# Six early chunks of a head-attention kernel: summing two tiles' products on TensorE and multiplying a third on VectorE

## The reference, cut to what matters

```python
q = (Q @ Wq.T + bq).reshape(n, ql, 16, 8)          # Q = layernorm(x)
k = (K @ Wk.T + bk).reshape(n, ql, 16, 8)          # K = V = context
v = (V @ Wv.T + bv).reshape(n, ql, 16, 8)
attn = softmax(einsum('nlhd,nled->nlhe', q, k) / sqrt(8), axis=-1)
ctx = einsum('nlhe,nled->nlhd', attn, v).reshape(n, ql, 128)
x = x + tanh(g) * (ctx @ Wo.T + bo)
```

## Time and profile before

| | |
|---|---|
| median of 3 runs | 1273.81 us (1272.21 to 1274.23) |
| the profiled execution | 1265.46 us, of which the span of the instructions is 1263.7 us |
| busy over the span | TensorE 89%, VectorE 76%, GpSimd 55%, ScalarE 54% |
| attention of the first six chunks | from 14.5 us (first product) to 227.1 us (first product of the seventh chunk) |
| 118.4 to 152.9 us, one chunk of these | TensorE busy 33.32, VectorE 32.16, GpSimd 33.12, ScalarE 14.84 of 34.50 us |
| 600 to 1260 us | TensorE busy 635.3 of 660 us |

### The profile page before, as it was taken

How to read it: one execution, slowest core, us unless ns; L and a number is a source line. 1 busy time by engine, 2 the same in 40 slices (tenths; PEclk the granted TensorE clock), 3 DMA queues, 4 the chain that set the end, 5 groups by cost and what they waited for, 6 DMA issues and landing times.

```text
span 1263.7 us, 23900 instructions
## 1 busy us (share of the span) xinstructions
PE 1124.9 (89%) x7368; PEld 965.1 (76%) x7368; DVE 957.1 (76%) x2069; ACT 682.0 (54%) x1939; POOL 692.6 (55%) x424
## 2 busy tenths in 40 slices
PE   5579974799889998896999999999999999999998
PEld 2356552688779887785989999999788888888886
DVE  4999999899999999988546444445867777777765
ACT  4434442466566765553564555555455555555554
POOL 6889997989899998988331010101133333333311
PEclk9975555799999999898899999999999999999999
DMA  3733432888779886877675566561111111111100
GB/s 109 241 116 126 133 109 93 250 251 250 238 226 280 258 251 206 245 246 223 204 240 163 167 185 187 186 191 61 34 33 34 34 35 35 33 35 34 33 9 18
DMA packets 134840, 183.34 MB, mean 145 GB/s; under 512 B 11293, under 2 KB 69176, under 8 KB 134714
## 3 DMA queue, kind: packets, MB, share of 16 engines
q1 hardware_dynamic: 129594, 169.22, 43.3%
q0 software_dynamic: 5120, 12.59, 2.9%
HBM read 146.10 MB, written 35.66 MB: 144 GB/s over the span
## 4 chain that ended last, share of the span: by engine, by line
PE 54%; DVE 26%; POOL 8%; issue 7%; ACT 3%; DMA 0%; DVEq 0%; POOLq 0%; ACTq 0%
PE ZB L1437 7%; DVE q_sb L1044 6%; PE YB L1451 6%; PE YD L1492 5%; DVE s L1019 4%; PE ZD L1403 4%; PE ZD L1405 4%; PE ZD L1404 4%; PE YB L1492 3%; POOL prod L635 3%; POOL prod L647 3%; PE ZB L1403 2%; DVE own_prod L1008 2%; DVE own_prod L1000 2%; PE ZB L1405 2%
## 5 line engine op out<-in xcount | busy, mean ns | idle before, releaser
L772 ACT ACTIVATE hid<-ZB,w2b 128x128 f32<-128x128 f32 x768 | 217.0, 374 | 110.2 <-PE YB L1451 72.5
L635 POOL TENSOR_TENSOR prod<-q_sb,kv_sb 128x2048 f32<-128x2048 f32 x48 | 216.0, 4502 | 36.6 <-DVE q_sb L1044 27.3
L1437 PE MATMUL ZB<-bt,w1b 128*128 128x128 f32 x1536 | 213.9, 284 | 23.8 <-ACT hid L772 17.9
L647 POOL TENSOR_TENSOR prod<-s,kv_sb 128x2048 f32<-128x2048 f32 x48 | 215.2, 4504 | 9.8 <-DVE q_sb L1044 9.6
L1437 PEld LDWEIGHTS ZB<-bt,w1b 128*128 128x128 f32 x1536 | 196.0, 199 | 29.8 <-issue 28.9
L622 POOL TENSOR_TENSOR rstd<-ve,neghalf 128x4 f32<-128x4 f32 x64 | 66.4, 1037 | 266.2 <-DVE ve L962 264.9
L679 POOL TENSOR_TENSOR own_prod<-own_prod,prod 128x512 f32<-128x512 f32 x44 | 56.5, 1284 | 205.3 <-ACT prod L804 205.3
L1451 PE MATMUL YB<-w2b,hid 128*128 128x128 f32 x1024 | 142.3, 283 | 0.0
L1246 DVE TENSOR_TENSOR prod<-own_prod,ZD 128x512 f32<-128x512 f32 x102 | 70.0, 686 | 93.4 <-ACT own_prod L794 52.1
L1451 PEld LDWEIGHTS YB<-w2b,hid 128*128 128x128 f32 x1024 | 130.5, 196 | 7.3 <-ACT hid L772 0.2
L794 ACT ACTIVATE own_prod<-ZD 128x512 f32<-128x512 f32 x102 | 61.0, 598 | 97.9 <-PE ZD L1405 97.3
(11 more groups left out here) (274 smaller groups left out, 2436.7 us busy)
## 6 DMA issues: line engine op xcount, KB each, us to landing
w2b<-in_w SPq DMA_DIRECT2D x96, 516.0 KB
w1b<-in_w SPq DMA_DIRECT2D x96, 512.0 KB, 4.9
xb<-xs SPq DMA_DIRECT2D x96, 128.0 KB, 3.4
ctx_t<-in_ctx SPq DMA_DIRECT2D x24, 256.0 KB, 3.1
x2d<-x2s SPq DMA_DIRECT2D x48, 128.0 KB, 5.0
x<-in_x SPq DMA_DIRECT2D x16, 256.0 KB, 3.6
xs<-zrow SPq DMA_DIRECT2D x4, 1024.0 KB, 6.0
xrow<-in_x SPq DMA_DIRECT2D x16, 256.0 KB, 5.1
```

Of the source, the lines that this page charges most:

```text
L635: pool.tensor_tensor(out=prod[:, t % 2, :].rearrange("p (h e d) -> p h e d", h=HEADS, e=HEADS), in0=q.unsqueeze(2).broadcast_to([P, HEADS, ...
L647: pool.tensor_tensor(out=prod[:, (t + 1) % 2, :].rearrange("p (h d e) -> p h d e", h=HEADS, e=HEADS), in0=s0[:, t, :, :].unsqueeze(2).broa ...
L772: act.activation(hid[n % 2][:, j, k * RT:(k + 1) * RT], ZB[j // 2][:, at:at + RT], ACT.Relu, bias=w2b[t % 3][:, k, e, FJ * D + j:FJ * D + ...
L1437: last = pe.matmul(ZB[j // 2][:, at:at + RT], w1b[t % 2][:, k, e, j * P:(j + 1) * P], bt[t % 2][:, k * RT:(k + 1) * RT], start=True, stop= ...
```

## The change

In the first six chunks (`EARLY = 6`):

- TensorE sums the products of tiles 0 and 1. It multiplies the slices of `prod` by the identity and lets PSUM add them up: for the scores 8 calls per tile on 256 columns each, taken 8 elements apart (`sum_scores`, at k = 3 and 5), for the outputs 16 calls per tile on 128 columns each, taken 16 elements apart (`sum_outputs`, at k = 11 and 12). All are full fp32 matmuls, which the program issues as two instructions each. The sums stand in ZD0 and ZD1.
- VectorE no longer sums these four. It takes maxima, subtraction and scaling of tiles 0 and 1 from PSUM, and does the first pair's maxima at k = 7 instead of k = 5 (ScalarE's exponential moves from k = 6 to k = 7).
- VectorE makes tile 2's product with the values (`second_times_v`) instead of GpSimd, from a copy of these values in YB, in `own_prod`, sums it, and then uses `own_prod` for tile 3. It adds a copy of 128 x 128 at k = 15.
- GpSimd makes five products per chunk instead of six. The two buffers alternate over the whole row of products.
- The languages stand at (0, 2, 7, 9) instead of (0, 2, 9, 12), and with them their loads and stores on SyncE.

The diff, cut to its core:

```diff
-LANG_AT = [16 * (c // 4) + 31 + (0, 2, 9, 12)[c % 4] for c in range(NC)]
+LANG_AT = [16 * (c // 4) + 31 + (0, 2, 7, 9)[c % 4] for c in range(NC)]
...
+EARLY = 6
+def product_buffer(a, i):
+    return (5 * a + i) % 2 if a < EARLY else i % 2
...
             def times_k(a, t):
                 if t == 2:
                     emptied(pool, "kv1", a)
-                    pool.wait_ge(score0.sem, score0.at(a, 1))
+                    if a < EARLY:
+                        pool.wait_ge(pe_sk.sem, pe_sk.at(a, 1))
+                    else:
+                        pool.wait_ge(score0.sem, score0.at(a, 1))
+                elif has(a - 1) and a - 1 < EARLY:
+                    pool.wait_ge(pe_sv.sem, pe_sv.at(a - 1, 1 + t))
...
             def times_v(a, t):
                 pool.wait_ge(exp0.sem, exp0.at(a, 1 + t // 2))
-                if t < 2:
+                if a < EARLY and t == 0:
+                    pool.wait_ge(pe_sk.sem, pe_sk.at(a))
+                elif t < 2:
                     pool.wait_ge(score0.sem, score0.at(a, 2 + t))
...
-                if k in (8, 10, 12) and has(a):
+                if k in (8, 10, 12) and has(a) and (a >= EARLY or k < 12):
                     times_v(a, k // 2 - 4)
...
+            def second_times_v(a):
+                dve.wait_ge(exp0.sem, exp0.at(a, 2))
+                dve.wait_ge(score0.sem, score0.at(a))
+                v = values_two.rearrange("p (d e) -> p d e", e=HEADS)
+                dve.tensor_tensor(out=own_prod[:].rearrange("p (h d e) -> p h d e", h=HEADS, e=HEADS),
+                                  in0=s0[:, 2, :, :].unsqueeze(2).broadcast_to([P, HEADS, HD, HEADS]),
+                                  in1=v.unsqueeze(1).broadcast_to([P, HEADS, HD, HEADS]),
+                                  op=ALU.mult).then_inc(two_av.sem, 1)
...
+            def sum_scores(a, t):
+                pe.wait_ge(pool_qk.sem, pool_qk.at(a, t + 1))
+                if has(a - 1):
+                    pe.wait_ge(sub0.sem, sub0.at(a - 1, 2))
+                src = prod[:, product_buffer(a, t), :].rearrange("p (g d) -> p g d", d=HD)
+                n = HEADS * HEADS
+                for d in range(HD):
+                    last = pe.matmul(pe_scores[:, t * n:(t + 1) * n], ident[:], src[:, :, d], start=(d == 0), stop=(d == HD - 1))
+                last.then_inc(pe_sk.sem, 1)
+
+            def sum_outputs(a, t):
+                pe.wait_ge(pool_av.sem, pool_av.at(a, t + 1))
+                if has(a - 1):
+                    pe.wait_ge(o_ready.sem, o_ready.at(a - 1, 1))
+                src = prod[:, product_buffer(a, 3 + t), :].rearrange("p (g e) -> p g e", e=HEADS)
+                for e in range(HEADS):
+                    last = pe.matmul(pe_outputs[:, t * D:(t + 1) * D], ident[:], src[:, :, e], start=(e == 0), stop=(e == HEADS - 1))
+                last.then_inc(pe_sv.sem, 1)
...
+                s, k = a_part(half)
+                if k in (3, 5) and 0 <= s < EARLY:
+                    sum_scores(s, k // 2 - 1)
+                if k in (11, 12) and 0 <= s < EARLY:
+                    sum_outputs(s, k - 11)
                 if half in LANG:
                     languages(LANG[half])
```

More of the change, by code:

```diff
@@ L368, in build @@
         sum_bank = [YB, ZD[1]]
+        pe_scores, pe_outputs, values_two = ZD[0], ZD[1], YB[:, 0:D]
         def tiles(b):
@@ L829, in _ @@
                     normed(0, lambda j: xn0[:, j, :], lambda j: x0[:, j, :], p, (0, 1) if k == 5 else (2, 3))
-                if k == 6 and has(a):
+                if k == 6 and a >= EARLY and has(a):
                     exp_heads(a, 0)
@@ L833, in _ @@
                     keys_values(p, 1)
+                if k == 7 and 0 <= a < EARLY:
+                    exp_heads(a, 0)
                 if half == 14:
@@ L1033, in head_sum @@
                 dve.wait_ge(exp0.sem, exp0.at(a, pair + 1))
+                if pair == 0 and a < EARLY:
+                    dve.tensor_reduce(out=rec0, in_=s0[:, ts, :, :].rearrange("p t h e -> p (t h) e"), axis=X, op=ALU.add).then_inc(rec0_s.sem, 1)
+                    dve.wait_ge(rec0_s.sem, rec0_s.at(a, 1))
+                    dve.reciprocal(rec_early[:], rec0).then_inc(rec0_s.sem, 1)
+                    return
                 dve.tensor_reduce(out=sum0[:, ts, :], in_=s0[:, ts, :, :], axis=X, op=ALU.add).then_inc(rec0_s.sem, 1)
@@ L1038, in head_out @@
             def head_out(a, t):
-                if t < PT:
+                second = t == 2 and a < EARLY
+                if second:
+                    dve.wait_ge(two_av.sem, two_av.at(a))
+                elif t < PT:
                     dve.wait_ge(pool_av.sem, pool_av.at(a, t + 1))
@@ L1042, in head_out @@
                     dve.wait_ge(own_av.sem, own_av.at(a))
-                src = prod[:, (t + 1) % 2, :] if t < PT else own_prod[:]
+                src = prod[:, (t + 1) % 2, :] if t < PT and not second else own_prod[:]
                 dve.tensor_reduce(out=o_sb[a % 2][:, t, :], in_=src.rearrange("p (g e) -> p g e", e=HEADS),
-                                  axis=X, op=ALU.add).then_inc(av_sum.sem, 1)
+                                  axis=X, op=ALU.add).then_inc(av_sum.sem, 3 if a < EARLY and t == 2 else 1)
             def head_scale(a, pair):
                 ts = slice(2 * pair, 2 * pair + 2)
-                dve.wait_ge(av_sum.sem, av_sum.at(a, 2 * pair + 2))
                 dve.wait_ge(rec0_s.sem, rec0_s.at(a, 2 * pair + 2))
                 o = o_sb[a % 2][:, ts, :].rearrange("p t (h d) -> p (t h) d", h=HEADS)
-                dve.tensor_tensor(out=o, in0=o, in1=rec0.unsqueeze(2).broadcast_to([P, 2 * HEADS, HD]),
+                if pair == 0 and a < EARLY:
+                    dve.wait_ge(pe_sv.sem, pe_sv.at(a))
+                    src, rec = pe_outputs[:, 0:2 * D].rearrange("p (g d) -> p g d", d=HD), rec_early[:]
+                else:
+                    dve.wait_ge(av_sum.sem, av_sum.at(a, 2 * pair + 2))
+                    src, rec = o, rec0
+                dve.tensor_tensor(out=o, in0=src, in1=rec.unsqueeze(2).broadcast_to([P, 2 * HEADS, HD]),
                                   op=ALU.mult).then_inc(o_ready.sem, 1)
@@ L1283, in _ @@
                     later_consts()
-                if k == 0 and has(r):
+                if k == 0 and r >= EARLY and has(r):
                     head_out(r, 2)
@@ L1292, in _ @@
                         variances_of_rows(p)
-                if k == 3 and has(a):
+                if k == 3 and a >= EARLY and has(a):
                     head_scores(a, 0)
-                if k == 4 and has(a):
+                if k == 4 and a >= EARLY and has(a):
                     head_scores(a, 1)
-                if k == 5 and has(a):
+                if k == 5 and a >= EARLY and has(a):
                     head_max(a, 0)
@@ L1302, in _ @@
                     norm_stats(1, lambda j: row[:, j, 0:D], r)
+                if k == 7 and 0 <= a < EARLY:
+                    head_max(a, 0)
                 if k == 7 and has(a):
@@ L1311, in _ @@
                     head_sum(a, 0)
-                if k == 11 and has(a):
+                if k == 11 and a >= EARLY and has(a):
                     head_out(a, 0)
@@ L1315, in _ @@
                     pick_group(r)
-                if k == 13 and has(a):
+                if k == 13 and a >= EARLY and has(a):
                     head_out(a, 1)
+                if k == 13 and 0 <= a < EARLY:
+                    second_times_v(a)
+                if k == 14 and 0 <= a < EARLY:
+                    head_out(a, 2)
                 if k == 14 and has(a):
```

35 lines of the change are left out of this document (26 added, 9 removed).

## The result

The changed kernel takes **1341.83 us** (median of 4 runs, 1339.86 to 1347.51) against 1273.01 us of the kernel before (4 runs, 1271.57 to 1274.23): ratio 1.0548, 95% interval 1.0513 to 1.0583. It is 69 us slower. The forecast was 1281 us; rival C, at 1342 us, is what came. The profiled execution took 1342.77 us, with a span of 1341.0.

What follows compares the result with a forecast made beforehand. GpSimd was taken to set the pace, 34.5 us per chunk. Start +1.3, two middle intervals +3.2 and the table interval +2.5 made +7 us, so the median 1273.8 became 1281 us; range 1258 to 1345.

Steps and rivals of the forecast that it cites:

- rival C: TensorE's sums read spaced columns at half speed at the high clock, 7.1 to 7.8 us each: +68, 1342 us; chance 0.14.
- case A: Main case: the forecast's sum of terms over the six chunks, +0 to +20 us, with borrowed sum prices; chance 0.57.
- The price of the sums: On TensorE at clock 1.00: 3.9 us per sum of scores, 3.6 per sum of outputs, 15 us per chunk.
- the ring: GpSimd and TensorE waiting on each other round a chunk: 19.8 + 16.3 = 36.1 us where it was 34.5, +1.6.
- The clock: TensorE's granted clock was taken as high (1.00) from the first chunk on, where it had been 0.50.
- D: Rival: TensorE's clock stays at 0.50, 61.7 us of work per chunk: +127, 1401 us; chance 0.09.
- K2: GpSimd's third key product, which may start only after TensorE's first sum of scores; predicted to wait about 6 us.
- the first two intervals: First to third chunk, where the pipeline still fills: no side seen to gain, put at 0.
- B: Rival: the ring closes in time and GpSimd's saving is kept: -13, 1261 us, or -32, 1242; chance 0.20.
- S0: TensorE's first sum of scores in a chunk, behind `ot` and `kv0`: 3.88 us and some 0.2 to drain.
- Moved languages at 0: Loads and stores of the moved languages on SyncE: put at 0, or a microsecond a chunk if cover went.
- The table chunk: Fifth to sixth chunk: 39.3 us against 39.7, but TensorE returns at the low clock, up to +5; taken as +2.5.

Runs made afterwards that it cites:

- x9: x7 with tile 2's product with the values back on GpSimd, TensorE summing as in x7: 1277.51 us, ratio 1.0015.
- x8: The changed kernel, spaced reading kept, with only the first sum of scores moved from k = 3 to k = 1: 1329.75 us, ratio 1.042.
- x3: The changed kernel with TensorE reading columns at a different spacing in each of the six chunks, from 1 to 8 (scores) or 16 (outputs): 1323.89 us.
- x1: The changed kernel with GpSimd writing products in another order, so TensorE's sums read neighbouring columns: 1293.42 us, ratio 1.0148.
- x5: x1 with the first sum of scores at k = 1 instead of 3, ahead of `ot` and `kv0`: 1271.26 us, ratio 0.9951.
- x7: x5 with VectorE's variances at k = 1, ahead of the last sum of outputs, instead of k = 2: 1268.39 us, ratio 0.9925.
- x4: The kernel before with only the languages moved, to (0, 2, 7, 9): 1273.6 us, ratio 0.9994.
- x10: x7 with the outputs of tiles 0 and 1 summed by VectorE again, TensorE summing only scores: 1303.86 us, ratio 1.0209.

## Why the prediction was right or wrong

The number was wrong, 1281 for 1342; the direction was right, and the range held the time only because it took in most of rival C, to which the prediction gave 0.14. Its main case A is not what happened.

- **What bounds the kernel before:** right. x9 gives GpSimd its sixth product back and the chunk is 34.7 us where the clock holds.
- **The price of the sums: the step that failed.** The prediction took 3.9 us for scores and 3.6 for outputs from dense rows, named them "a lower bound of cost if spacing hurts", and gave the spaced case 0.14. They measured 7.4 and 7.0. The diff itself had the warning: every column of the new calls lies in a 16-byte line of its own, and no row of such a read stood beside it. A row of the same shape with another layout is a bound, not a price; the sum took the bound as the value, and 0.14 was too little for C.
- **C's working:** TensorE's work "49 us per chunk, which then sets the pace". Measured 46.8 busy of 47.9, and x8 shows that this load, not the ring, holds the chunk. "14.7 more in four intervals, some 9 for the first and last" became 53.1 and 15.7, 68.8 for 68. The mechanism was C's, but that its sum met the time to a microsecond is partly luck: one term was 5.7 too large and the other 6.7 too small. "Half speed" had no row behind it either; x3 is what shows it.
- **The clock:** right. It reads 1.00 in the middle chunks, 0.50 before; D fell.
- **Case A on its own ground (x1):** the mechanism was right, its sum was short. The ring was put at 36.1 us and K2's wait at 6.0; measured 36.7 and 4.5. But the whole came to +19 where +7 was summed. From K2 to K2, as the prediction counts, the profiled executions show the terms: the start gained 2.2 (put at +1.3; 1.3 of the gain is this execution's earlier begin), the first two intervals lost 5.0 and 5.3 (put at 0, although they hold the same ring and K2 waits 7.8 and 6.1 us in them), the next two 1.8 and 2.1 for 1.6 each, the one with the table 5.4 for 2.5. That is +17; the rest lies behind the six chunks or in what one execution differs from the next. "I find no side that gains and take 0" was a term not worked out.
- **B, the place where it could turn:** right place, and not reached by cheaper sums; those cost 3.45 us, near the dense rows. S0 earlier in TensorE's order closes the ring (x5), and the variances after that (x7).
- **Moved languages at 0:** right (x4). **PSUM reads and the copy:** the copy is 0.24 us, maxima and subtraction 0.69 each from either memory. **GpSimd's products:** 4.5 us each as before.
- **The table chunk:** `ot` stands behind VectorE's table as said; in after TensorE idles 7.85 us there, comes back at a granted clock of 0.50, and K2 waits 10.07.
- **The chances** hold a slip: the cases as priced give 0.14 for the same and 0.65 for slower, not 0.15 and 0.64. Nothing hangs on it.

## What to carry to other kernels

Before you price a matmul from a row of the same shape, compare how its operands lie in memory: a moving operand (the one that streams through the array, here the products) whose fp32 columns lay four or more elements apart ran at half speed at the high clock, and it was free here to let GpSimd write in the order in which TensorE reads. When work leaves the full engine, walk the ring that the freed engine now closes, and put the instruction it waits for as early in the other engine's order as its inputs allow; that line was worth 22 us here, and the layout 48. Adding 4.5 us to an engine with room (VectorE, busy 25.9 of 33.1 us) can cost more than its own length if it lands ahead of what another engine waits for: x10 has 27 us of such sums and took 35 us more than x7.

## What the runs showed of the hardware that was not expected

- In these full fp32 matmuls, at a granted clock of 1.00, TensorE reads at 1.76 ns per 16-byte line per partition, and at 0.84 ns per column if columns share lines; the slower of the two decides (x3). At the low clock the spacing is hidden, as far as the rows show: four dense instructions of 256 columns take 1.87 us there, 7.5 for sixteen (an estimate), and the spaced sum of the changed kernel behind the table, begun at a granted clock of 0.50 that held for its first 2 us, took 7.58, where the others take 7.54. Cheaper sums begun at 0.50 do lose by it: one with neighbouring columns took 5.53 for 3.62 (x10), one at step 2 took 4.47 for 3.79 (x3).

```profile
261.90 2.08 PE L1462 MATMUL MC<-ws,ctx_t 128*128 128x256 f32 x4
263.77 7.58 PE L1616 MATMUL ZD<-prod,ident 128*128 128x256 f32 x16
```

- GpSimd writes fp32 elements 1 KB (scores) or 512 bytes (outputs) apart as fast as neighbours: two products of 2048 take 9.05 and 9.03 us in x1, one takes 4.48 to 4.55 in the changed kernel.
- The clock can fall at a wait of under 2 us. In x1 the 64 instructions of two output sums in a row took 8.87 us instead of twice 3.7. The windows over that stretch and its second part read 0.83 and 1.00 for the granted clock:

```profile
153.90:163.00 9.10, 9.07 (x68) 9.07 (x69) 8.76 (x12) 1.80 (x9) 8.09 (x2) 0.83 0.17 53
159.00:163.00 4.00, 4.00 (x39) 4.00 (x38) 3.86 (x3) 0.00 (x0) 3.63 (x1) 1.00 0.00 0
```

Microsecond by microsecond it reads 0.50 from 153.9, where the stretch begins, to 157.0, and 1.00 from there. TensorE had waited 1.76 us for GpSimd just before; the sum at 117.61, behind a wait of 1.94, took 3.84 us at a granted clock of 1.00. What decides between the two was not tried.
